# First attention: query and key projections as three fp32r products of split operands, list positions in bf16, loop over rows written out

## The reference

```python
h = layernorm(x) * (1 + ca) + sa
q = h @ w_q;  kv = h @ w_kv              # 128 -> 16 heads x 64; keys are also the values
q, kv = rotate(q), rotate(kv)            # kv*cos + rotate_half(kv)*sin
# local keys: windows of 128, own and previous, normalised over 64 features
# pooled keys: a softmax-weighted mean of every 16 keys, normalised
att = softmax([q.pooled, q.local] + mask) @ [pooled, local]
x = x + ga * (att @ w_out + b_out)
h = layernorm(x) * (1 + cb) + sb
weights, experts = top_2(h @ router_w)   # of 4 experts
x = x + gb * experts_of(h)
```

## Time and profile before

| | us |
|---|---|
| median of 3 runs (lowest, highest) | 1512.7 (1509.84, 1518.84) |
| the profiled execution: device time, span of the core | 1513.62, 1511.8 |
| TensorE busy (share of the span) | 1200.5 (79%) |
| VectorE busy | 931.4 (62%) |
| ScalarE busy | 822.3 (54%) |
| GpSimd busy | 725.5 (48%) |
| mean granted TensorE clock | 0.896 |

### The profile page before, as it was taken

The page is one execution under the profiler, slowest core; times in us unless marked ns, Lnnn a source line. Parts: engine busy times, 40 slices in busy tenths (PEclk is TensorE's granted clock), DMA queues, the critical chain, the costliest instruction groups (busy, mean ns, idle before and its releaser), DMA issues. The chain is left out here.

```text
span 1511.8 us, 30131 instructions
## 1 busy us (share of the span) xinstructions
PE 1200.5 (79%) x9299; PEld 928.5 (61%) x9299; DVE 931.4 (62%) x2122; ACT 822.3 (54%) x2181; POOL 725.5 (48%) x750
## 2 busy tenths in 40 slices
PE   3368988989889993898899899889937887888436
PEld 1245665656656662898899889889913444444336
DVE  4687787787876533744744664764434677776633
ACT  1256777767677771676676666666612443344101
POOL 2646748567485312565566556556653323211223
PEclk8589999989998995999999999999966999899558
DMA  7500000000000003303003000000063445331145
GB/s 221 174 2 3 1 10 3 8 10 0 9 2 8 10 8 127 124 11 125 8 11 120 16 9 10 12 12 7 10 174 81 84 87 104 58 48 21 23 121 152
DMA packets 152775, 76.43 MB, mean 51 GB/s; under 512 B 99992, under 2 KB 143384, under 8 KB 152408
## 3 DMA queue, kind: packets, MB, share of 16 engines
q1 hardware_dynamic: 144696, 66.42, 16.8%
q0 software_dynamic: 3072, 6.31, 1.3%
q10 hardware_dynamic: 4896, 2.36, 0.5%
HBM read 54.77 MB, written 19.76 MB: 49 GB/s over the span
## 5 line engine op out<-in xcount | busy, mean ns | idle before, releaser
L1477 POOL TENSOR_TENSOR hl<-hid,hh 128x256 fp32r<-128x256 f32 x396 | 294.0, 744 | 218.8 <-ACT hh L1454 215.1
L1520 DVE SCALAR_TENSOR_TENSOR hid<-GU,gub,sg 128x256 f32<-128x256 f32 x396 | 190.5, 482 | 194.7 <-ACT sg L1448 123.5
L1348 PE MATMUL GU<-xh,wh 128*128 128x256 f32 x792 | 233.3, 295 | 39.4 <-DVE wl L1496 30.3
L1448 ACT ACTIVATE sg<-GU,gub 128x256 f32<-128x256 f32 x396 | 188.1, 475 | 123.6 <-PE GU L1350 121.7
L1349 PE MATMUL GU<-xl,wh 128*128 128x256 f32 x792 | 225.3, 284 | 0.0
L1350 PE MATMUL GU<-xh,wl 128*128 128x256 f32 x792 | 225.1, 284 | 0.0
L1348 PEld LDWEIGHTS GU<-xh,wh 128*128 128x128 f32 x792 | 152.1, 192 | 49.0 <-issue 27.3
L1454 ACT CAST hh<-hid 128x256 fp32r<-128x256 f32 x396 | 158.2, 399 | 25.8 <-DVE hid L1520 25.3
L1349 PEld LDWEIGHTS GU<-xl,wh 128*128 128x128 f32 x792 | 152.5, 193 | 0.0
L1350 PEld LDWEIGHTS GU<-xh,wl 128*128 128x128 f32 x792 | 152.2, 192 | 0.0
L648 ACT ACTIVATE prob<-prob,rZ 128x272 f32<-128x272 f32 (+1 forms) x256 | 98.9, 462 | 60.6 <-DVE rZ L1021 55.2
(11 more groups left out here) (312 smaller groups left out, 2842.6 us busy)
## 6 DMA issues: line engine op xcount, KB each, us to landing
raw<-in_expert_w SPq DMA_DIRECT2D x4, 2688.0 KB, 12.0
late<-in_w SPq DMA_DIRECT2D x20, 256.0 KB, 6.1
raw<-in_expert_w SPq DMA_DIRECT2D x4, 1152.0 KB, 6.1
list<-zero SPq DMA_DIRECT2D x4, 1024.0 KB, 8.6
modb<-mod_d SPq DMA_DIRECT2D x9, 384.0 KB, 4.3
early<-rel_d SPq DMA_DIRECT2D x1, 3072.0 KB, 13.1
qkv_d<-qkv SPq DMA_DIRECT2D x48, 64.0 KB
early<-in_w SPq DMA_DIRECT2D x12, 256.0 KB, 4.2
```

What stands on the lines that cost most here:

```text
L1348: pe.matmul(out, lhs[0], rhs[0], start=start, stop=False, skip_group_check=True)
L1448: act.activation(sg[:, c % BUFS], GU[c % BUFS][:, 0:TT], ACT.Silu, bias=gub[:, GATE, e * CH0 + c:e * CH0 + c + 1]).then_inc(silu, 1)
L1477: pool.tensor_tensor(hl[:, b], hid[:, b], hh[:, b].bitcast(F32), ALU.subtract).then_inc(hid_lo, 1)
L1520: dve.scalar_tensor_tensor(out=hid[:, c % BUFS], in0=GU[c % BUFS][:, TT:2 * TT], scalar=gub[:, UP, e * CH0 + c:e * CH0 + c + 1], in1=sg[:, ...
```

## The change

- Operands of the query and key projections are split in two fp32r parts, high (the value rounded to fp32r) and low (the rest), and each product becomes three: high x high, high x low, low x high, summed in PSUM (`three`). The weights are split once in the prologue: ScalarE rounds (`wkvh`, `wqh`), VectorE subtracts (`wkvl`, `wql`). The fp32 weights are landed in tiles that are not in use yet (`attT`, `pT`).
- The row is split in step 4 of every `norm` slot: ScalarE writes `hTh` and `hkv` from A1, VectorE subtracts into `hTl` (`input_low`). Three buffers by row; the copy `hT` in step 7 is gone. `kv_mm` waits for the low part (`hq`) and the weights' low part (`w_low`).
- `both`, `seen` and the matrices `before` and `ones` of `pos_mm` are bf16 (small whole numbers).
- `over_slots` writes all slots straight. Waits are on constants.
- `modb`, the modulation sent to all partitions, holds 3 of its 6 parts; a few semaphores are merged.

```diff
-def over_slots(eng, slot_program):
-    slot_program(-2, 0)
-    slot_program(-1, 1)
-    slot_program(0, 0)
-    slot_program(1, 1)
-    with eng.Fori(0, 2) as j:
-        slot_program(2 * j + 2, 0)
-        slot_program(2 * j + 3, 1)
-    for slot in range(6, NB + 1):
+def over_slots(slot_program):
+    for slot in range(-2, NB + 1):
         slot_program(slot, slot % 2)
...
-        hT = sb("hT", [P, 2, NT])
+        hTh = sb("hTh", [P, 3, NT], F32R)
+        hTl = sb("hTl", [P, 3, NT], F32R)
...
+        wq = attT[:].rearrange("p c q -> p (c q)").rearrange("p (s n) -> p s n", s=2)
+        wkv = pT[:].rearrange("p a e q -> p (a e q)")[:, 0:INNER]
...
-        both = sb("both", [P, TILES, E0])
-        seen = sb("seen", [P, TILES + 1, E0])
+        both = sb("both", [P, TILES, E0], BF16)
+        seen = sb("seen", [P, TILES + 1, E0], BF16)
...
+            def three(out, lhs, rhs):
+                pe.matmul(out, lhs[0], rhs[0], start=True, stop=False, skip_group_check=True)
+                pe.matmul(out, lhs[0], rhs[1], start=False, stop=False, skip_group_check=True)
+                return pe.matmul(out, lhs[1], rhs[0], start=False, stop=True, skip_group_check=True)
...
             def kv_mm(slot, t, n):
+                b = slot + 2
                 if t == 0 and n == 0:
-                    bank1.wait_emptied(pe, "hT", slot)
+                    pe.wait_ge(hq, b + 1)
+                    pe.wait_ge(w_low, 1)
                 bank, a = use(f"kv{t}{n}", slot)
-                pe.matmul(a[:], hkv[:, t * P:(t + 1) * P], wkv[:, n * 512:(n + 1) * 512],
-                          start=True, stop=True).then_inc(bank.full, 1)
+                tokens, cols = slice(t * P, (t + 1) * P), slice(n * 512, (n + 1) * 512)
+                three(a[:], (hTh[:, b % 3, tokens], hTl[:, b % 3, tokens]), (wkvh[:, cols], wkvl[:, cols])).then_inc(bank.full, 1)
...
                 for s in range(2):
-                    mm = pe.matmul(Q[:, s * NT:(s + 1) * NT], wq[:, s, hp * P:(hp + 1) * P], hT[:, bp, :],
-                                   start=True, stop=True)
+                    mm = three(Q[:, s * NT:(s + 1) * NT], (wqh[:, s, cols], wql[:, s, cols]), (hTh[:, b % 3, :], hTl[:, b % 3, :]))
...
                 for t in range(TILES):
-                    pe.matmul(a[:, t * E0:(t + 1) * E0], cst("before"), both[:, t, :], start=True, stop=False)
-                    mm = pe.matmul(a[:, t * E0:(t + 1) * E0], cst("ones"), seen[:, t, :], start=False, stop=True)
+                    pe.matmul(a[:, t * E0:(t + 1) * E0], beforeb[:], both[:, t, :], start=True, stop=False)
+                    mm = pe.matmul(a[:, t * E0:(t + 1) * E0], onesb[:], seen[:, t, :], start=False, stop=True)
...
+            act.wait_ge(w_in, 16 * n_w)
+            act.copy(wkvh[:], wkv).then_inc(w_high, 1)
...
-                        act.activation(hkv[:], A1[:, 0:NT], ACT.Identity, bias=modT[:, MSA, bass.ds(r, 1)],
-                                       scale=modT[:, MCA, bass.ds(r, 1)]).then_inc(bank1.drained, 1)
+                        if r >= 1:
+                            act.wait_ge(hq, r)
+                        if r >= 3:
+                            act.wait_ge(q_mm, HP * (r - 2))
+                        for to in (hTh[:, r % 3, :], hkv[:]):
+                            i = act.activation(to, A1[:, 0:NT], ACT.Identity, bias=modT[:, MSA, r:r + 1], scale=modT[:, MCA, r:r + 1])
+                        i.then_inc(bank1.drained, 1)
...
-                    if norm and hp == 7:
-                        if not known_zero(r - 1):
-                            act.wait_ge(q_mm, HP * (r - 1))
-                        act.copy(hT[:, bp, :], hkv[:]).then_inc(hq, 1)
+                    if slot == -1 and hp == 3:
+                        act.wait_ge(wq_in, 16 * n_wq)
+                        act.copy(wqh[:], wq).then_inc(w_high, 1)
...
+            def input_low(slot, r):
+                bank1.wait_emptied(dve, "hT", slot)
+                dve.tensor_tensor(hTl[:, r % 3, :], hkv[:], hTh[:, r % 3, :].bitcast(F32), ALU.subtract).then_inc(hq, 1)
...
+                    if slot == -2 and hp == 3:
+                        dve.wait_ge(w_high, 1)
+                        dve.tensor_tensor(wkvl[:], wkv, wkvh[:].bitcast(F32), ALU.subtract).then_inc(w_low, 1)
+                    if norm and hp == 4:
+                        input_low(slot, r)
                     if early and hp == 4:
                         pooled_norm(slot, b)
+                    if slot == -1 and hp == 5:
+                        dve.wait_ge(w_high, 2)
+                        dve.tensor_tensor(wql[:], wq, wqh[:].bitcast(F32), ALU.subtract).then_inc(w_low, 1)
```

More of the change, by code:

```diff
@@ L121, in index @@
     def index(self, name, slot):
-        every = [x for x, _ in self.order]
-        if not isinstance(slot, int):
-            return (slot - 2) * len(every) + self.index(every[0], 2) + every.index(name)
         n = 0
@@ L217, in layer0_attention @@
         xt = sb("xt", [P, NB * TILES, D])
-        modb = sb("modb", [P, NB, 6 * D])
+        modb = sb("modb", [P, NB, 3 * D])
         modT = sb("modT", [P, 5, NB])
@@ L375, in pooled_values @@
                 take_waits(sp, taken)
-            pooled_values(0, 0)
-            pooled_values(1, 1)
-            with sp.Fori(0, (NB - 2) // 2) as j:
-                pooled_values(2 * j + 2, 0)
-                pooled_values(2 * j + 3, 1)
+            for b in range(NB):
+                pooled_values(b, b % 2)
             sp.wait_ge(filled, 16 * (E0 + 2))
@@ L578, in slot_program @@
                         hT_mm(slot, slot + 2)
-                    if isinstance(slot, int) and slot == -1 and hp == HP - 1:
+                    if slot == -1 and hp == HP - 1:
                         pe.wait_ge(wq_in, 16 * n_wq)
@@ L614, in slot_program @@
                         pos_mm(slot, slot - 1)
-            over_slots(pe, slot_program)
+            over_slots(slot_program)
             pe.wait_ge(t_step, T_STEPS * NB)
             pe.wait_ge(q_rot, NB * HP)
-            pe.matmul(Q[:, 0:E0], cst("ones"), seen[:, TILES, :], start=True, stop=True).then_inc(count_mm, 1)
+            pe.matmul(Q[:, 0:E0], onesb[:], seen[:, TILES, :], start=True, stop=True).then_inc(count_mm, 1)
         @block.scalar
@@ L689, in slot_program @@
                     if heads:
-                        if not (isinstance(n, int) and n < 2):
+                        if n >= 2:
                             act.wait_ge(pT_mm, n - 1)
@@ L704, in slot_program @@
                         act.wait_ge(pT_mm, m + 1)
-                        if not (isinstance(m, int) and m < 2):
+                        if m >= 2:
                             act.wait_ge(o_mm, m - 1)
@@ L1028, in slot_program @@
                         rotate_queries(n + 1, (hp + 1) % 2)
-                    if isinstance(slot, int) and slot == 0 and hp == 0:
+                    if slot == 0 and hp == 0:
                         dve.wait_ge(w_in, 16 * n_w)
@@ L1035, in slot_program @@
                         kv_center(b, 1)
-                    if norm and hp == 0 and not (isinstance(slot, int) and slot == -2):
+                    if norm and hp == 0 and not (slot == -2):
                         layernorm1(r)
@@ L1088, in _ @@
             dve.tensor_copy(identb[:], ident).then_inc(cast, 1)
+            dve.tensor_copy(beforeb[:], cst("before"))
+            dve.tensor_copy(onesb[:], cst("ones"))
             dve.tensor_copy(maskb[:], cst("mask")).then_inc(cast, 1)
-            over_slots(dve, slot_program)
+            over_slots(slot_program)
             dve.wait_ge(count_mm, 1)
@@ L1217, in slot_program @@
                         swap_rotate(slot, r, 1)
-                        if isinstance(slot, int) and slot == -2:
+                        if slot == -2:
                             pool.wait_ge(w_in, 16 * n_w)
```

52 lines of the change are left out of this document (28 added, 24 removed).

## The result

| | us |
|---|---|
| kernel before, median of 20 (lowest, highest) | 1517.28 (1507.23, 1527.67) |
| changed kernel, median of 20 (lowest, highest) | 1506.57 (1500.12, 1514.90) |
| ratio, 95% interval | 0.9928 (0.9909 to 0.9946) |
| profiled execution of the changed kernel: device time, span | 1505.21, 1503.4 |

The change gains 10.7 us, between 8 and 14. The prediction was 1500 with a sum of -13.1. Rare executions far above the rest (1656 us in e12, 1073 us in e11) stand in no ratio and in no median here. In the two profiled executions the last instruction of the first attention's routing (`ntiles` on VectorE) starts at 582.1 us before and 575.0 after, 7.1 us earlier; the spans are 8.4 us apart.

What follows compares the result with a forecast made beforehand. VectorE was taken to bound most steps, with TensorE passes counting only in step 0 and where no VectorE work runs beside. Terms sum to -13.1 us from 1513.62, giving 1500.5, called 1500; range 1486 to 1509.

Steps and rivals of the forecast that it cites:

- Step 0: Slots 2 to 6: VectorE's waits for scores and queries (1.21 us) go, -6.1; slot 1: shorter queries, -0.5.
- rival B: TensorE stays at the lower clock longer; slow scores of step 1 would give 1506 us; chance 0.22 together with D.
- Steps hidden behind VectorE: Steps 1 to 3 and 5 to 7, slots 1 to 5: shorter products hidden, 0; slot 0 gains, -0.5 us.
- Step 4: Slots 0 to 5: ScalarE's extra tile costs 0.45 us, key products return 0.42, subtraction falls in idle time; +0.2.
- Loop: Loop written straight: stall at slot 4 goes, -1.6 us; fewer register instructions where VectorE bounds, -1.3.
- Slots 6 and 7: No `norm` work, so saved TensorE passes count: slot 7 -2.0 us, slot 6 -1.0 beyond its step 0 gain.
- End of routing: VectorE's wait of 1.96 us for the last `pos_mm`, with nothing beside it, gets shorter: -1.2 us.
- Prologue: Splitting before the first key product delays slot 0, +0.9 us; wq's split costs 0, or +2 at half VectorE pace.
- Rival C: Slower by code loading: straight slots stall 3 us at a time, two in each of four slots making 1524; chance 0.06.
- Rival A: TensorE is the bound throughout, so all saved passes count: -34, 1479 us; chance 0.12.
- D: Step 0 gives nothing, as something else is late behind the removed waits: -7, 1506 us; chance 0.22 together with rival B.

Runs made afterwards that it cites:

- e12: Whole kernel before with the loop written out and positions in bf16, all projections fp32; 1509.39 us, ratio 0.9965 to the kernel before.
- e11: Kernel before, cut behind the first attention, with loop written out, bf16 positions and 14 unread TensorE products ahead of the positions; 590.15 us.
- e4: Whole changed kernel with 14 unread bf16 products added in TensorE's idle time ahead of the positions, slots 0 to 6; 1511.56 us, ratio 0.9981.
- e6: Changed kernel cut behind the first attention, nothing else changed; 589.25 us.
- e3: Whole changed kernel with the subtraction for wq's low part moved later in slot -1; 1507.52 us, ratio 0.9943 to the kernel before.
- e1: Whole kernel before with slots 2 to 5 written straight, nothing else changed; 1519.63 us, ratio 0.9991.
- e10: Kernel before, cut behind the first attention, with loop written out and bf16 positions, all projections fp32; 587.31 us.
- e2: Whole changed kernel with VectorE making the row's low part straight from PSUM in two instructions; 1507.76 us, ratio 0.9929 to the kernel before.
- e8: Changed kernel, cut behind the first attention, with the row's low-part subtraction placed behind VectorE's two reads of A0 in step 4; 592.88 us.
- e9: Changed kernel, cut behind the first attention, with keys projected in fp32 again and only the queries split; 586.93 us.
- e5: Kernel before cut behind the first attention, loop kept; 598.19 us.
- e7: Kernel before, cut behind the first attention, with slots 2 to 5 written straight; 594.43 us.

## Why the prediction came out right, step by step

The total was right (-13.1 against -10.7, inside the interval) with the wrong parts: the largest term came to nothing, two costs were too small, and what made up for them was in part not forecast. That the sum came out near is luck in part.

1. *Step 0, -6.6 forecast, about nothing found; the largest step that failed.* Both waits went, as forecast, but I had asked only what VectorE does next and not what TensorE does next. TensorE goes through step 0 at the lower clock, so the scores of step 1 are late in their turn (0.81), and step 0 of slots 2 to 6 takes 7.43 us in the mean, where it took 7.46. That was rival B's step, with about its price of 1 us a slot; e4 shows the other side, 6.5 us at full clock. The sum was also too large at the start: it takes slot 5 for all of slots 2 to 6, but before, the waits stand in slots 3, 5 and 6 (1.11, 1.21 and 1.31 us) and not in slot 2. Slot 1, forecast at -0.5, got 1.6 us longer in step 0 (7.36 to 8.93; it varies by execution, 8.12 in e6 and 7.12 in e3). As for the wait for S, it is gone in four of five slots of e1, where the positions are still fp32, and stays with 0.96 us in one. In no trace with bf16 positions does it stand in slots 2 to 6. So the loop and `pos_mm` both had a part in it.
2. *Steps hidden behind VectorE, -0.5.* Steps 2 and 3 are 0.16 us shorter each against e1 and e10, in every slot. A shorter query product shows there, but steps 4 and 5 give it back, since GpSimd had not got further. The cover was complete in slots 1 to 5; only it was GpSimd as well as VectorE.
3. *Step 4, +0.2 forecast, mis-sized.* It reads "VectorE's subtraction (about 0.4 us) falls into its idle time". It took 2.12 us, and step 4 grew by 1.27. Step 5 gave back 0.34 and step 6 another 0.36; with steps 2 and 3, 0.2 us a slot remain, 1.0 us over slots 1 to 5 where the sum had 0.03 a slot. In e2, e8 and e9 the sum of steps 4 and 5 stayed at 19.1 to 19.3: the cost is not its place on VectorE or what waits for it there, but by how much it holds up GpSimd. What the sum did not have at all is the 1.7 us of slot 2, where the clock fell in step 4 (steps 4 and 5 took 20.99 us there against 19.25). The key products themselves cost what I took, 0.73 for 0.65 forecast.
4. *Loop, -2.9.* -3.8 by the cut medians (e5, e7), with runs that overlap; -1.4 by the ratio of the whole kernel, with an interval that holds zero. Stall and register instructions went, and TensorE's own register instructions with them.
5. *Slots 6 and 7, -3.0.* In slot 7, steps 2, 3, 5 and 6 gave 0.16 each, and the last count of positions but one came 0.7 us earlier. The 1.78 of step 0 is the wait of 3.07 us, which is 1.44 after. I had read that wait as a stall of straight code and left it in. e1 does not have it (step 0 of slot 7 falls from 6.54 to 4.90), but neither does e5, which keeps the loop. So it stands in one of two traces with the loop and in none of eleven without, and what it came from stays open. The split products do give something in slot 7: from its first to its last maxima it is 37.6 us in the changed kernel and 38.5 in e10 and e12, 0.9 us, where I had forecast 1.6. Another 2.5 us lie behind slot 7, where no term of mine was: before, the last values and the output projection ran in part at the lower clock (its 32 products start over 5.19 us), in the changed kernel they did not (3.56). That varies by execution: e6 and e12 have the 3.56 as well, e5 and e10 5.2 to 5.3, and e8, a variant of the changed kernel, 5.87. So this part of the gain is luck of the two profiled executions.
6. *End of routing, -1.2.* The last wait for positions fell from 1.96 to 0.36 us, -1.6.
7. *Prologue, +0.9 forecast, 2.9 found.* This step failed too. Counted from the first `hT_mm`, the first key product starts 1.6 us later, and e9 shows what that hands on to slot 0: 0.9. The other 2.0 come with the split of the queries. I had +2 as the upper end, for half pace. The subtraction for wq took 3.05 us, ahead of the variance of the pooled keys, but its place there is not the reason: e3 moved it and slot 0 did not start earlier. What on the chain it holds up stays open.

Rival C is refuted: in the straight slots neither VectorE nor ScalarE nor TensorE's products have a stall without a releaser above 0.3 us. The rule that straight code hides its fetching (the Trainium skill, page Runtime: NRT & Kernel Launch, section Instruction fetch mechanics) agrees with this; the wait in slot 7 that I held against it is in no trace of straight code. Rival A is refuted by 61.6 us a slot, not 58. Rivals B and D were right that step 0 gives nothing, B with the right mechanism; the late thing was the scores and not a product of GpSimd. Their 1506 was worked out as -7 from 1512.7; measured are -10.7, nearer to the forecast's -13.1.

What the whole change gives is, by the cut kernels, the loop (3.8 us) and the bf16 positions (7.1 us by the medians of e7 and e10, 5.0 by their ratios, since the chips differ). Of the positions' part the traces place two pieces in every pair: the last wait but one fell from 2.18 to 1.47 us and the last from 1.96 to 0.36, 2.3 us in all. A wait of 0.95 us for the scores, which e1 and e7 have in one slot each, is gone as well. The rest moves with where the stretches at the lower clock fall: between e7 and e10 3.6 us lie ahead of slot 7, between e1 and e12 only 0.8. The three fp32r products, on which the change spends most of its lines, give by the cut kernels between nothing and a loss of 2 us; the whole kernels lean the other way.

Open: why the whole kernels rank e12 behind the changed one; what the split of wq holds up in the prologue; and what would hold TensorE's clock up without a cost elsewhere. Taking the subtraction off VectorE altogether wasn't tried.

## What to carry to other kernels

When a wait goes, follow both engines one step further: what was next may be as late. Where GpSimd works without a gap, look whether it sets the pace: time saved ahead of it is then taken back, and an instruction added beside it costs what it holds up GpSimd (0.2 us here), not how long it looks (2.12) and not its own 0.4. Before a later start or an earlier end is put down to an edit, look at something ahead of the edit: it may have moved as much. And time a part of a program by itself when the rest varies by more than the change.

## What was not expected of the hardware

- VectorE's fp32 instruction on 256 columns took 0.4 to 2.12 us by what GpSimd was doing. It ended 0.28 us after GpSimd's instruction, and GpSimd's next one was then about 0.2 us longer: 2.56 for 2.35 behind the subtraction, 2.08 for 1.90 behind `qr`. The one that read PSUM took 0.47 in the same place. One with a single SBUF operand (`tensor_scalar`) was stretched to 1.48.
- The lower clock of a slot's start followed idle time of TensorE (1.80 us ahead of the positions, 1.71). In slot 2 of the changed kernel it came in step 4 too, after a wait of 1.53 us for `h2T`; slots 3 to 5 waited as long and kept the full clock. Before, with 0.74 there, slots 1 to 6 had no low stretch in step 4. Filling an idle stretch moved the low stretch to another step in e4.
- A product of 128x512 in fp32r took 0.23 us at full clock, the same per column as one of 256 (0.118). At the lower clock, four bf16 products of 4 columns took 0.24 us up to the next product, where eight fp32 passes took 1.72 with register instructions behind them.
